# Phase 1 of a window mixer with routed experts: scatters regrouped between the powers on GpSimd, places and two Gelus moved forward, the block lists computed in three pieces

## What is computed

```python
# _mamba, over the 49 places of a window
h = xb + h @ A                # xb = layernorm(x) @ Bm
xr = h @ Cm
# the MLP of the block, and the first residual
y = gelu(layernorm(xr) @ W1 + b1) @ W2 + b2
x = x + xr + y
# routed experts, top 2 of 4
t = x;  n = layernorm(t)
probs = softmax(n @ gate_w + gate_b)
masked = probs * mask_of_top2;  masked /= sum(masked) + 1e-9
out = t + sum_e masked[e] * (gelu(n @ w1[e] + b1[e]) @ w2[e] + b2[e])
```

## Time and profile before

| | us |
|---|---|
| median of three runs | 1870.0 |
| lowest, highest | 1868.61, 1870.57 |
| span of the profiled execution | 2018.7 |
| busy in it: PE, DVE, ACT, POOL | 1868.9, 1528.0, 1472.7, 1387.6 |

### The profile page before, as it was taken

How to read it: one execution, slowest core, us unless ns; L and a number is a source line. 1 busy time by engine, 2 the same in 40 slices (tenths; PEclk the granted TensorE clock), 3 DMA queues, 4 the chain that set the end, 5 groups by cost and what they waited for, 6 DMA issues and landing times.

```text
span 2018.7 us, 35592 instructions
## 1 busy us (share of the span) xinstructions
PE 1868.9 (93%) x8486; PEld 1266.7 (63%) x8486; DVE 1528.0 (76%) x6498; ACT 1472.7 (73%) x2823; POOL 1387.6 (69%) x1097
## 2 busy tenths in 40 slices
PE   5988898898988898898999799999999999999997
PEld 3545555554545455554577577777777777777775
DVE  6787778777777778777688677777777777777775
ACT  2666566665656566656699688998888888888886
POOL 3466666666666667666677678888777777777776
PEclk9999999999999899999999899999999999999999
DMA  6253323333333333332466666677666766766663
GB/s 178 87 151 103 111 88 114 94 111 91 107 89 112 92 107 111 96 99 62 154 200 200 218 194 213 208 219 214 207 202 200 213 201 202 211 209 211 199 205 101
DMA packets 139737, 312.03 MB, mean 155 GB/s; under 512 B 35066, under 2 KB 43925, under 8 KB 139530
## 3 DMA queue, kind: packets, MB, share of 16 engines
q1 hardware_dynamic: 104424, 249.10, 42.2%
q0 software_dynamic: 32000, 58.87, 8.4%
q10 hardware_dynamic: 3106, 1.78, 0.4%
HBM read 243.43 MB, written 67.19 MB: 154 GB/s over the span
## 4 chain that ended last, share of the span: by engine, by line
PE 49%; POOL 26%; issue 23%; DVE 1%; ACT 1%; DMA 0%; POOLq 0%; ACTq 0%; DVEq 0%
POOL sorted_rows L522 17%; PE mix_ps L1291 7%; PE mix_ps L1293 7%; PE mix_ps L1292 7%; POOL rstd_xt L511 7%; PE up_ps L1277 4%; PE turn_ps L1277 4%; PE up_ps L1278 4%; PE turn_ps L1278 4%; PE up_ps L1279 3%; PE turn_ps L1279 3%; PE tok_ps L1302 3%; PE y_ps L1214 2%; POOL rows L519 1%; PE y_ps L1166 0%
## 5 line engine op out<-in xcount | busy, mean ns | idle before, releaser
L573 POOL DMA_INDIRECT out<-out_sb,idx x412 | 436.3, 1059 | 242.9 <-DVE out_sb L1074 127.5
L1033 DVE TENSOR_TENSOR g_lo<-g,g_hi 128x512 fp32r<-128x512 f32 x618 | 422.2, 690 | 197.1 <-ACT g_hi L702 127.9
L522 POOL DMA_INDIRECT sorted_rows<-rows,pos x392 | 386.6, 986 | 155.8 <-issue 102.6
L1166 PE MATMUL y_ps<-g,d_mlp 128*100 128x512 f32 x588 | 325.3, 651 | 72.4 <-ACT g L633 72.3
L702 ACT CAST g_hi<-g 128x512 fp32r<-128x512 f32 x618 | 381.5, 617 | 13.1
L549 POOL TENSOR_TENSOR ex<-euler,rows 128x16 f32<-128x16 f32 x103 | 307.7, 2987 | 0.6
L1291 PE MATMUL mix_ps<-g_hi,ew 128*96 128x512 f32 x618 | 245.0, 396 | 0.5 <-issue 0.3
L1293 PE MATMUL mix_ps<-g_lo,ew 128*96 128x512 f32 x618 | 244.7, 396 | 0.0
L1292 PE MATMUL mix_ps<-g_hi,ew 128*96 128x512 f32 x618 | 244.1, 395 | 0.0
L498 POOL TENSOR_TENSOR rstd_r<-var_eps,neg_half 128x8 f32<-128x8 f32 x49 | 81.8, 1669 | 213.5 <-DVE var_eps L815 213.5
L633 ACT ACTIVATE g<-up_ps 128x512 f32<-128x512 f32 x294 | 161.7, 602 | 77.9 <-PE up_ps L1159 67.3
(11 more groups left out here) (185 smaller groups left out, 4009.7 us busy)
## 6 DMA issues: line engine op xcount, KB each, us to landing
ew<-expert_w SPq DMA_DIRECT2D x206, 384.0 KB
ew<-expert_w SPq DMA_DIRECT2D x206, 288.5 KB
rows<-sorted_rows SPq DMA_DIRECT2D x103, 394.0 KB
x_in<-in_x SPq DMA_DIRECT2D x49, 384.0 KB, 3.1
x_raw_t<-in_x_chan SPq DMA_DIRECT2D x49, 384.0 KB
rstd_t<-rstd_rows SPq DMA_DIRECT2D x49, 384.0 KB
out<-out_sb,idx POOLq DMA_INDIRECT x412
sorted_rows<-rows,pos POOLq DMA_INDIRECT x392
```

The lines of the kernel that those rows point to most:

```text
L522: pool.indirect_dma_start(out=sorted_rows[:, :], out_offset=bass.IndirectOffsetOnAxis(ap=pos[:, r, s:s + 1], axis=0), in_=rows[:, r, s, :] ...
L573: pool.indirect_dma_start(out=out_rows, out_offset=bass.IndirectOffsetOnAxis(ap=idx[:, r, s:s + 1], axis=0), in_=out_sb[:, r, s, :], in_of ...
L1033: dve.tensor_tensor(g_lo[:, n % PART_RING, :], g[:, n % G_RING, :], f(g_hi[:, n % PART_RING, :]), ALU.subtract).then_inc(lo_done, 1)
L1166: pe.matmul(y_ps[0:CG, :], d_mlp[:, k, :], g[:, n % G_RING, :], start=(k == 0), stop=(k == KB - 1)).then_inc(down_done, 1)
```

## The change

What it does, engine by engine:

- GpSimd: the power over two halves becomes two, `rstd_of_x` (into `rstd_x`) and `rstd_of_rows` (into `rstd_n`). The eight scatters of a tile are no longer 4 + 4 but 2 + 3 + 3 (`SCATTER_AT`), each group with a power ahead of it. The wait for `h_summed` is gone, and the column of row numbers goes to VectorE (into `positions`, with its wait `id_ok`). In phase 2, 19 scatters are left over.
- VectorE: `positions` moves from behind `shift_of_r` to ahead of the statistics of `mix_ps`; the statistics of the input from there to behind `shift_of_r`; `deviation_of_x` to ahead of it, one period later than before (for tile `p+2`). `list_blocks` has three parts: for the first list part 0 in period 45 ahead of the statistics of `mix_ps`, parts 1 and 2 in period 46 around the statistics of the input and `scale_x`; for the second list part 0 after block 10, parts 1 and 2 within block 11.
- ScalarE: Gelus 4 and 5 move ahead of the first half of `normalise_xr`.

```diff
+SCATTER_AT = (2, 5)
+LEFT = SUBS - SCATTER_AT[1] + 2 * SUBS
...
             for p in periods():
                 if tile(p - 3):
-                    if tile(p + 1):
-
-                        pool.wait_ge(h_summed, p + 2)
-                    scatter(p - 3, range(HALF_SUBS, SUBS))
+                    scatter(p - 3, range(SCATTER_AT[1], SUBS))
                 if tile(p + 1):
                     rstd_of_r(p + 1)
-                if tile(p + 3) or tile(p - 1):
-                    rstd_of_x_and_t(p + 3)
                 if tile(p - 2):
-                    scatter(p - 2, range(HALF_SUBS))
+                    scatter(p - 2, range(SCATTER_AT[0]))
+                if tile(p - 1):
+                    rstd_of_rows(p - 1)
+                if tile(p - 2):
+                    scatter(p - 2, range(SCATTER_AT[0], SCATTER_AT[1]))
+                if tile(p + 3):
+                    rstd_of_x(p + 3)
...
-                if tile(r):
-                    normalise_xr(r, 0)
                 if tile(p):
                     gelu(p, 4)
                     gelu(p, 5)
                 if tile(r):
+                    normalise_xr(r, 0)
                     normalise_xr(r, 1)
...
+                dve.tensor_scalar(rows[:, t % ROW_RING, :, COL_ID], ids0[:, :], 1.0, float(t * TOK), ALU.mult, ALU.add)
                 dve.wait_ge(ranked, t + 1)
...
-                if tile(p + 3):
-                    t = p + 3
-                    dve.wait_ge(x_loaded[t % X_RING], 16 * (t // X_RING + 1))
-                    in_stats(LN_X, t, lambda s: x_in[:, t % X_RING, s, :])
-                    variance(LN_X, t, (rstd_xt_ok, t))
+                if tile(p - 2):
+                    positions(p - 2)
+                if p == KNOWN + 2:
+                    dve.wait_ge(base_set, KNOWN + 1)
+                    list_blocks(0, 0)
...
                     take_xr(r)
+                if tile(p + 2) and p >= 0:
+                    deviation_of_x(p + 2)
+                if tile(r):
                     shift_of_r(r)
                 if p == KNOWN + 3:
-                    dve.wait_ge(base_set, KNOWN + 1)
-                    list_blocks(0)
-                if tile(p - 2):
-                    positions(p - 2)
+                    list_blocks(0, 1)
+                if tile(p + 3) and p >= 0:
+                    stats_of_x(p + 3)
                 if tile(p + 2):
                     scale_x(p + 2)
+                if p == KNOWN + 3:
+                    list_blocks(0, 2)
...
                     if u == 5 and b == 10:
                         dve.wait_ge(base_set, TILES)
-                        list_blocks(1)
+                        list_blocks(1, 0)
+                    if u == 2 and b == 11:
+                        list_blocks(1, 1)
+                    if u == 5 and b == 11:
+                        list_blocks(1, 2)
```

More of the change, by code:

```diff
@@ L497, in rstd_of_r, with rstd_of_x, rstd_of_rows @@
                     pool.wait_ge(xr_n_ok, t - 1)
[L498 to L507, removed]
-                    pool.wait_ge(rstd_saved, 16 * (t - 1))
[L509 to L512, removed]
+                pool.tensor_tensor(rstd_r[:, t % 2, :], var_eps[:, LN_R, :], neg_half[:, :], ALU.pow).then_inc(rstd_r_ok, 1)
+            def rstd_of_x(t):
+                pool.wait_ge(var_ok[LN_X], t + 1)
+                if t >= 2:
+                    pool.wait_ge(rstd_saved, 16 * (t - 1))
+                    pool.wait_ge(dev_ok, t - 1)
+                pool.tensor_tensor(rstd_x[:, t % 2, :], var_eps[:, LN_X, :], neg_half[:, :], ALU.pow).then_inc(rstd_x_ok, 1)
+            def rstd_of_rows(t):
+                pool.wait_ge(var_ok[LN_T], t + 1)
+                if t >= 2:
+                    pool.wait_ge(t_n_ok, t - 1)
+                pool.tensor_tensor(rstd_n[:, t % 2, :], var_eps[:, LN_T, :], neg_half[:, :], ALU.pow).then_inc(rstd_n_ok, 1)
             def scatter(t, subs):
@@ L552, in left_scatter @@
             def left_scatter(i):
[L554 to L559, removed]
+                t, n = TILES - 3, i + SCATTER_AT[1]
+                scatter(t + n // SUBS, range(n % SUBS, n % SUBS + 1))
             powers(0)
@@ new lines, in list_blocks @@
+                if part == 0:
+                    dve.tensor_tensor(found[:, :], base[:, :], tau7[:, 0:TYPES], ALU.subtract).then_inc(list_step, 1)
+                    after(1)
+                    dve.scalar_tensor_tensor(over[:, :, :], in0=wide(found[:, :].unsqueeze(2), [P, TYPES, N // BLK]),
+                                             scalar=float(2 - BLK if run == 0 else 1), in1=steps512[:, :, :], op0=ALU.add,
+                                             op1=ALU.is_gt).then_inc(list_step, 1)
+                    after(2)
+                    dve.tensor_reduce(n_blk[:, 0:TYPES], over[:, :, :], AX_X, ALU.add).then_inc(list_step, 1)
@@ new lines, in list_blocks @@
+                if part == 1:
+                    after(3)
+                    dve.tensor_tensor(rest[:, :], n_blk[:, :], taken[:, :], ALU.subtract).then_inc(list_step, 1)
+                    after(4)
+                    dve.tensor_tensor_scan(last_blk[:, :], ones[:, 0:TYPES + 1], rest[:, :], 0.0, ALU.mult, ALU.add).then_inc(list_step, 1)
+                    after(5)
+                    dve.tensor_tensor(first_blk[:, :], last_blk[:, :], rest[:, :], ALU.subtract).then_inc(list_step, 1)
+                    after(6)
+                    dve.tensor_scalar(nth[:, :], first_blk[:, :], -1.0, part_no[:, run:run + 1], ALU.mult, ALU.add).then_inc(list_step, 1)
+                    after(7)
+                    dve.tensor_tensor(mine[:, :], nth[:, :], rest[:, :], ALU.is_lt).then_inc(list_step, 1)
+                    after(8)
+                    dve.scalar_tensor_tensor(mine[:, :], in0=nth[:, :], scalar=0.0, in1=mine[:, :], op0=ALU.is_ge,
+                                             op1=ALU.mult).then_inc(list_step, 1)
+                    dve.tensor_tensor(shifted[:, :], nth[:, :], taken[:, :], ALU.add).then_inc(list_step, 1)
```

115 lines of the change are left out of this document (49 added, 66 removed).

## The result

The changed kernel takes 1915.7 us (median of four runs, 1914.4 to 1917.4), the kernel before 1869.5 us in the same session. The ratio is 1.025, with a 95% interval from 1.0238 to 1.0263: slower by 46 us, where 6 us of gain were forecast.

What follows compares the result with a forecast made beforehand. TensorE's own 16.59 us a period was taken to bound the runs in phase 1. Gelus 2, second list 2.7 and first list 1.7 summed to 6.4 us, 1870.0 to 1864 us; the 8-in-10 range was 1836 to 1882.

Steps and rivals of the forecast that it cites:

- late release: Phase 1: TensorE's finished `sum_xr` reaches VectorE 2 us late during eight scatters; claimed to come from tracing, hardly in the runs.
- a subtraction: Phase 1 period: the profile's 148.7 us excess over the median, spread on 45 periods, leaves 16.53 us, TensorE's own pace.
- The launch work: Around the kernel: 9 to 15 us by the Trainium skill, making a period 0.2 to 0.3 us less.
- VectorE's loop of 16.4 to 16.5 us: VectorE's phase 1 period after the change, summed from starts plus the row-number column; claimed still under TensorE's 16.59.
- TensorE's 16.59: TensorE's own work in a phase 1 period, 17.16 us less one wait of 0.57; taken as the runs' pace.
- the price of the scatters: GpSimd's loop: three powers of 1.67 and eight scatters of 1.32, 15.6 to 15.9 us against 16.5; worth 0.
- the rule weighed: Trainium skill: two-SBUF-input VectorE and SBUF-reading GpSimd instructions lock each other out; claimed not borne out by the row.
- Rival 4: Phase 1: `x_t` and a power lock each other out, costing VectorE 1.5 us a period, 68 us, 1930; chance 0.04.
- Rival 3: Phase 1: GpSimd becomes the bound, through power-scatter gaps or a waiting scatter; 18 us, 1884 (1875 to 1900); chance 0.14.
- The places sooner: VectorE, phase 1: places ahead of the statistics of `mix_ps` remove TensorE's 0.49 us wait for `base`; worth 0 in the runs.
- Gelus and lists: Earlier Gelus 4 and 5: 0.05 us a period, 2 us; lists in pieces: 1.7 us for the first, 2.7 for the second.
- The sign "no wait over 2 us at the lists": Profile after the change: TensorE should show no wait above 2 us where VectorE makes the two lists.

Runs made afterwards that it cites:

- one_ahead: The changed kernel with one scatter instead of two between `rstd_r` and `rstd_n` (`SCATTER_AT = (1, 4)`); 1860.3 us, ratio 0.9954 to the kernel before.
- places_late: `one_ahead` with the places, and the first part of the first list, put back behind `shift_r`; 1914.7 us.
- x_t_later: The changed kernel with `x_t` moved behind the sum x2 of the tile's first half on VectorE, so `rstd_n` starts first; 1868.8 us.
- three_ahead: The changed kernel with three scatters instead of two between `rstd_r` and `rstd_n` (`SCATTER_AT = (3, 6)`); 1996.3 us.
- four_ahead: The changed kernel with four scatters instead of two between `rstd_r` and `rstd_n` (`SCATTER_AT = (4, 7)`); 2102.1 us.

## Why the prediction was wrong

**The runs don't have the late release: right.** The step went by a subtraction, 19.83 - 3.30 = 16.53 us, and the kernel before, taken again, has 16.53. It held because nearly all of the excess lies in phase 1: the last `rstd_r` starts at 975.1 us there and at 831.6 in the profile taken again, 143.5 of the 151.1 us between the two spans. The reason given, that tracing the scatters makes it, was wrong: with the same run of eight scatters the recorded rows show none of it. What disturbed that one execution stays open. The launch work that the prediction brought in has no part in it: the runs stand 1.7 us over their spans (1869.3 and 1867.6, 1914.4 and 1912.7).

**VectorE's loop of 16.4 to 16.5 us: right,** as far as it went. In the changed kernel `y_lo` follows `y_lo` at 17.56 us, of which 1.09 are the new wait: 16.47. TensorE's 16.59 was 0.1 too long: in `one_ahead` it waits 1.3 us in the whole stretch from 120 to 760 us, and the period there is (794.5 - 101.8) / 42 = 16.49.

**The step that failed is the price of the scatters,** "3 x 1.67", and the rule weighed. I took 1.67 us for a power wherever it stands, and set the lock-out aside by one row of the kernel before: a power that starts at 601.29 and `x_t` at 602.58, neither longer. The row is sound and has the wrong order in it. The power had started first, and in that order nothing is held, as `one_ahead` shows again. In the changed kernel `x_t` starts first, by 0.21 us, and the power takes 3.36. The order was to be had beforehand from my own terms: `rstd_r`, its 1.67 and two scatters of 1.3 put `rstd_n` some 4.3 us behind the start of `rstd_r`, and `shift_r` at 1.70 with the statistics of x, 2.16, put `x_t` at 3.9. Two numbers 0.4 apart, with a row for one order only, were a case to be priced, not to be left out.

**Rival 4 had the mechanism and the wrong victim.** It let VectorE pay 1.5 us a period and gave it a chance of 0.04. GpSimd pays: the hold is 3.36 - 1.67 = 1.69 us, of which 0.6 lies in VectorE's own work behind `x_t`, and 1.09 comes through. 45 x (17.56 - 16.53) = 46 us, as much as the runs lost. In the profiles the last `rstd_r` starts 47.5 us later than in the kernel before (879.1 and 831.6), and what follows it is 2.4 us shorter.

**Rival 3 didn't come true in the changed kernel.** GpSimd's loop without what is held and what idles is 17.56 - 1.69 - 0.79 = 15.1 us, under my 15.6 to 15.9. But its mechanism, a scatter that waits for its places, is what `places_late` shows.

**The places sooner: right as to the sum, wrong as to what they are for.** "Worth 0" holds for the whole; the term should have said that the scatters' new order needs them, at 54 us (1914.7 against 1860.3).

**Gelus and lists: right in size.** The Gelus were forecast at 2 us, and 2.6 were measured, hardly clear of noise. The lists were forecast at 2.7 + 1.7 = 4.4, and 6.6 were measured. By TensorE's waits, `one_ahead` against the kernel before, the second list fell from 2.3 to nothing and the first from 2.62 to 1.13: 2.3 of the 2.7 and 1.5 of the 1.7. The sign "no wait over 2 us at the lists" failed in the changed kernel, where the one of 2.22 has the new wait of each period in it.

## What to carry to other kernels

When a GpSimd instruction moves next to a long VectorE instruction that works from SBUF on both sides, work out which of the two starts first: in one order the overlap was free, in the other GpSimd's was held until VectorE's had ended, and one scatter's length decided between 1860 and 1916 us. Put something nobody waits for (here a scatter) into the held place, and leave more than a few tenths of a microsecond between the starts. A profile whose span is far from the runs should not be read for waits before it has been set against them.

## What the runs showed of the hardware

- A hold lasts to the end of the VectorE instruction inside which GpSimd's begins. Then a power still took 1.53 to 1.55 us and a scatter 0.85 to 0.93, nearly their whole plain length, after an `x_t` of 2.02, 1.09 or 0.69 us.
- It meets scatters too: in the rows read 1.46 (`x_t_later`) to 2.43 us (`four_ahead`) instead of 0.96 to 1.04. On this the Trainium skill ("SBUF — State Buffer", Who interferes with whom) infers that a `tensor_tensor` doesn't stall the writing of descriptors; here the scatter's instruction, which reads its places from SBUF, is held by one, and the measurement decides. Which part of the scatter is held, the reading of its places or the writing of descriptors, no row tells.
- The other way round nothing was held: `x_t` took 2.02 us in `one_ahead` although it began inside a power. The same section of the Trainium skill says of VectorE's 2-port modes that whoever issues first gets the shared ports for the whole instruction, and the other blocks fully; these runs, most of them with a `tensor_tensor` of two inputs, show a hold only for VectorE ahead of GpSimd.
- Waits of 0.86 us a period left TensorE's granted clock at 1.00 (the changed kernel). With waits of up to 2.1 us (`three_ahead`) it was 0.91 over the stretch, and with waits of up to 3.3 us (`four_ahead`) 0.86; at the lower level a product takes 0.63 us instead of 0.39. It fell behind some of these waits and not behind others of the same length.
